# A post-norm decoder layer with a mixture of experts: expert weights split into f16 parts during the attention batches

## What is computed

```python
gate_probs = softmax(x @ gate_w + gate_b)
weights, selected = top_k(gate_probs, 2)
weights = weights / sum(weights)
comb = zeros((n, 8)).at[arange(n)[:, None], selected].set(weights)
h = gelu(einsum('nd,edf->enf', x, w1) + b1[:, None, :])      # w1: 8 x 256 x 1024
expert_out = einsum('enf,efd->end', h, w2) + b2[:, None, :]  # w2: 8 x 1024 x 256
out = einsum('ne,end->nd', comb, expert_out)
```

## Time and profile before

| | before |
|---|---|
| runs, us | 880.97, 886.6, 889.96 (median 886.6) |
| profiled execution, us | 884.88 |
| its span, us | 883.1 |
| mean granted TensorE clock | 0.982 of full speed |
| PE busy | 800.3 us (91%) |
| PEld busy | 608.1 us (69%) |
| DVE busy | 632.6 us (72%) |
| ACT busy | 511.2 us (58%) |
| POOL busy | 260.6 us (30%) |
| chain that ended last | PE 40%, DMA 29%, DVE 10%, SP's queue 7%, ACT 7% |

### The profile page before, as it was taken

One profiled execution on the slowest core, in us unless ns is written; L12 is line 12 of the kernel. 1 busy time (PEld: TensorE's weight loads), 2 busy tenths in 40 slices (PEclk: granted clock), 3 DMA queues, 4 the chain that ended last, 5 costly groups with the idle time before them and its releaser, 6 DMA issues.

```text
span 883.1 us, 30182 instructions
## 1 busy us (share of the span) xinstructions
PE 800.3 (91%) x12379; PEld 608.1 (69%) x12379; DVE 632.6 (72%) x1234; ACT 511.2 (58%) x1084; POOL 260.6 (30%) x334
## 2 busy tenths in 40 slices
PE   5689998999999989999899999999997789999996
PEld 3356766666666666666676666767665569999995
DVE  5866776768777767776777778776864736588887
ACT  2336655666566546655665665656664443687782
POOL 4233223222612251225123421522240103133332
PEclk9999999999999999999999999999999789999999
DMA  7355544554555554554555555545466855766653
GB/s 220 108 149 160 159 137 133 152 164 131 160 148 147 160 149 128 163 152 143 148 151 156 153 158 158 172 136 160 138 190 177 294 195 182 215 202 184 205 155 95
DMA packets 91377, 143.25 MB, mean 162 GB/s; under 512 B 11423, under 2 KB 79583, under 8 KB 87918
## 3 DMA queue, kind: packets, MB, share of 16 engines
q1 hardware_dynamic: 87742, 136.74, 51.8%
q0 software_dynamic: 3504, 4.62, 2.7%
HBM read 101.60 MB, written 39.68 MB: 160 GB/s over the span
## 4 chain that ended last, share of the span: by engine, by line
PE 40%; DMA 29%; DVE 10%; SPq 7%; ACT 7%; issue 5%; DVEq 0%; POOLq 0%; POOL 0%; ACTq 0%
DMA k_dram<-k_two 15%; DMA sums<-y_sb,g_token 9%; PE ps L1613 8%; PE ps L1606 7%; PE ps L1687 5%; SPq L1079 5%; PE ps L1665 4%; DMA k_st<-k_dram 4%; ACT k_two L1368 3%; DVE k_two L507 3%; PE ps L1629 3%; PE ps L1923 3%; DVE negmax L513 2%; PE ps L1944 2%; PE ps L1697 2%
## 5 line engine op out<-in xcount | busy, mean ns | idle before, releaser
L513 DVE TENSOR_REDUCE negmax<-ps 112x1 f32<-112x1500 f32 x121 | 207.3, 1713 | 44.4 <-PE ps L1629 44.1
L1395 ACT ACTIVATE pT<-ps 125x448 f32<-125x448 f32 x384 | 195.8, 546 | 18.6 <-PE ps L1665 14.7
L1230 POOL TENSOR_TENSOR ctx_lo<-ctx_raw,ctx_hi 128x250 f16<-128x250 f32 x188 | 119.3, 666 | 229.7 <-DVE ctx_hi L498 212.8
L1665 PE MATMUL ps<-qbd,k_st 97*128 97x112 f16 x1536 | 129.4, 216 | 20.2 <-ACT qbd L1351 10.8
L1665 PEld LDWEIGHTS ps<-qbd,k_st 97*128 97x128 f16 x1536 | 92.9, 99 | 78.0 <-ACT qbd L1351 27.1
L507 DVE SCALAR_TENSOR_TENSOR k_two<-ps,bk_sb,k_two 128x500 f16<-128x500 f32 x96 | 70.7, 736 | 96.7 <-ACT k_two L1368 96.7
L1368 ACT ACTIVATE k_two<-ps,bk_sb 128x500 f16<-128x500 f32 x96 | 65.1, 678 | 91.6 <-PE ps L1606 68.6
L1351 ACT COPY v_sb<-ps 125x512 f32<-125x512 f32 x96 | 56.3, 587 | 89.5 <-PE ps L1613 89.4
L1687 PE MATMUL ps<-pT,v_sb 125*17 125x56 f32 x6144 | 93.4, 217 | 10.1 <-issue 10.1
L1687 PEld LDWEIGHTS ps<-pT,v_sb 125*17 125x17 f32 x6144 | 81.5, 100 | 29.5 <-issue 19.2
L1629 PE MATMUL ps<-k_st,qbd 96*112 96x500 f16 x363 | 97.4, 375 | 3.7 <-DMA k_st<-k_dram 2.9
(11 more groups left out here) (258 smaller groups left out, 1396.0 us busy)
## 6 DMA issues: line engine op xcount, KB each, us to landing
k_st<-k_dram SPq DMA_DIRECT2D x288, 125.0 KB, 2.6
w_sb<-w SPq DMA_DIRECT2D x25, 1024.0 KB, 5.1
ctx_raw<-ctx_T SPq DMA_DIRECT2D x48, 500.0 KB, 4.5
k_dram<-k_two SPq DMA_DIRECT2D x96, 250.0 KB, 3.6
xs<-zeros SPq DMA_DIRECT2D x28, 260.0 KB, 3.1
w_sb<-w SPq DMA_DIRECT2D x8, 512.0 KB, 4.9
xg<-xs SPq DMA_DIRECT2D x21, 130.0 KB, 4.1
a_x<-x_tok SPq DMA_DIRECT2D x8, 128.0 KB, 2.8
```

The lines of the kernel that those rows point to most:

```text
L513: V.tensor_reduce(negmax[0:QW], ps[0:QW, BANK_S:BANK_S + CHUNKS, 0:MC], AX.XY, ALU.max, negate=True).then_inc(max_done, 1)
L1230: last = nc.gpsimd.tensor_tensor(ctx_lo[:, k, c2, a], ctx_raw[:, k, c2, a], ctx_hi[:, k, c2, a], ALU.subtract)
L1395: nc.scalar.activation(pT[0:MT, (PAIRS * b + p) % 3, TPC * g:TPC * g + TPC], ps[0:MT, BANK_T + n % 2, 0:TPC * QW].rearrange("p (t n) -> p ...
L1665: last = mm(ps[:, BANK_T + n % 2, QW * i:QW * i + QW], k_st[:, j, p, a:a + P], qbd[:, j, p].rearrange("p h s -> p (h s)"), start=True, sto ...
```

## The change: what it does

**Splitting in the batches.** `w1` and `w2` are cut into 32 pieces of 128 x 1024 (`PIECES`). POOL loads a piece (`load_piece`, 512 KB), rounds 32 times its value to f16 (`round_piece`), DVE makes the f16 remainder (`rest_of_piece`), and POOL stores both parts to DRAM (`store_piece`, 512 KB, into `w1_parts` or `w2_parts`). Five pieces go through in each of the first pairs of batches, at slots 2, 4, 8, 10 and 15. There are two buffers for the raw piece, and one, `w_hl`, for its parts: a piece is rounded only when the store of the one before has landed.

**f16 products.** Both layers of every expert tile are sums of three f16 products (high with high, high with low, low with high). The rows are split by DVE into `xgT_hi` and `xgT_lo`, the hidden values by ACT and DVE into `h_hi` and `h_lo`, now for all 21 tiles. `w2_hi_step`, `w2_lo_step` and the f32 second layer are gone. The factor 32 is divided out in the gelu and in the gate.

**Two sums.** Even expert tiles are added to `sums`, odd ones to `sums_odd`; an addition waits for the last one to the same tensor. `sums_odd` is set to zero in the batches, one 128-row tile at a time on SP's queue, loaded at the end into `acc_odd`, and carried into the banks by four more f32 products, two ahead of the last second layer and two behind it.

**Loads.** `w1` has three buffers, and its load waits for the tile three back. In the last batch the loads of `w2` parts are issued between the store of the keys and the wait for it, not behind the loads of the keys. The order of the first five expert tiles on PE and DVE is written anew.

```diff
@@ POOL @@
+            def round_piece(n):
+
+                if n < len(PIECES):
+                    pool.wait_ge(raw_in[n % 2], 16 * (n // 2 + 1))
+                    if n > 0:
+                        pool.wait_ge(w_parts_out, 16 * n)
+                    nc.gpsimd.tensor_scalar(w_hl[:, 0], w_raw[:, n % 2], W_UP, None, ALU.mult).then_inc(w_hi_made, 1)
+
+            def store_piece(n):
+
+                if n < len(PIECES):
+                    of, e, i = PIECES[n]
+                    pool.wait_ge(w_lo_made, n + 1)
+                    nc.gpsimd.dma_start((w1_parts if of == 1 else w2_parts)[e, i],
+                                        w_hl[:].rearrange("p i n -> p (i n)")).then_inc(w_parts_out, 16)
+                if n + 2 < len(PIECES):
+                    load_piece(n + 2)
...
             def add(g):
                 pool.wait_ge(row_read, g + 1)
                 pool.wait_ge(y_ready, g + 1)
-                if g > 0:
-                    pool.wait_ge(added, 16 * g)
+                if g > 1:
+                    pool.wait_ge(added[g % 2], 16 * (g // 2))
...
@@ DVE @@
+            def rest_of_piece(n):
+
+                if n < len(PIECES):
+                    dve.wait_ge(w_hi_made, n + 1)
+                    V.scalar_tensor_tensor(w_hl[:, 1], w_raw[:, n % 2], W_UP, w_hl[:, 0], ALU.mult, ALU.subtract).then_inc(w_lo_made, 1)
...
-                V.tensor_copy(xgT[:, g % 2], ps[:, XG_BANK, 0:D].rearrange("p (c n) -> p c n", c=CH)).then_inc(xgT_done, 1)
+                src = ps[:, XG_BANK, 0:D].rearrange("p (c n) -> p c n", c=CH)
+                V.tensor_copy(xgT_hi[:, g % 2], src).then_inc(xgT_done, 1)
+                dve.wait_ge(xgT_done, 2 * g + 1)
+                V.tensor_tensor(xgT_lo[:, g % 2], src, xgT_hi[:, g % 2], ALU.subtract).then_inc(xgT_done, 1)
...
@@ SP @@
-            def keys(b, par, u):
+            def keys(b, par, u, between=()):
...
                 sp.dma_start(k_dram[i], k_two[:, i]).then_inc(k_out[g], 16)
+                for dst, src in between:
+                    sp.dma_start(dst, src).then_inc(w2_in, 16)
                 sp.wait_ge(k_out[g], 16 * (CHUNKS * b + c + 1))
...
-                if g >= 2:
-                    sp.wait_ge(m1_done, 2 * g - 2)
+                if g >= 3:
+                    sp.wait_ge(m1_done, 2 * g - 4)
...
@@ PE @@
                 for q in range(4):
                     f = 4 * i + q
-                    for c in range(CH):
-                        last = mm(ps[:, H_BANK + 2 * par + i, P * q:P * q + P],
-                                  w1_sb[:, par, c, P * f:P * f + P], xgT[:, par, c],
-                                  start=(c == 0), stop=(c == CH - 1))
+                    for n, (x, w) in enumerate(SPLIT):
+                        for c in range(CH):
+                            last = mm(ps[:, H_BANK + 2 * par + i, P * q:P * q + P],
+                                      w1_place(g)[:, c, F * w + P * f:F * w + P * f + P], (xgT_hi, xgT_lo)[x][:, par, c],
+                                      start=(n == 0 and c == 0), stop=(n == 2 and c == CH - 1))
...
+                pe.wait_ge(h_lo_done, g + 1)
                 for f in range(FT):
...
+                    for n, (x, w) in enumerate(SPLIT):
+                        a = F * w + D * (f % 4)
+                        last = mm(ps[:, Y_BANKS[par], 0:D], (h_hi, h_lo)[x][:, par, f],
+                                  w2_sb[:, bass.ds(e, 1), f // 4, a:a + D].rearrange("p a n -> p (a n)"),
+                                  start=(f == 0 and n == 0), stop=(f == FT - 1 and n == 2))
...
+            for q in (2, 3):
+                carried_odd(q)
+            m2(GT - 1)
```

More of the change, by code:

```diff
@@ L360, in decoder_layer @@
         row_made = sem("row_made")
-        w2_hi_done = sem("w2_hi_done")
-        w2_lo_done = sem("w2_lo_done")
+        raw_in = [sem(f"raw_in{k}") for k in range(2)]
+        w_hi_made = sem("w_hi_made")
+        w_lo_made = sem("w_lo_made")
+        w_parts_out = sem("w_parts_out")
+        odd_in = sem("odd_in")
         h_hi_done = sem("h_hi_done")
@@ L376, in decoder_layer @@
         b2_in = sem("b2_in")
-        added = sem("added")
+        added = [sem(f"added{k}") for k in range(2)]
         gate_step = sem("gate_step")
@@ L417, in decoder_layer, with w1_place @@
         C_FREE = (9 - UNITS, 0, 4)
+        PIECE_AT = {2: 0, 4: 1, 8: 2, 10: 3, 15: 4}
         W2_AHEAD = (1, 2, 1, 1, 2, 1)
+        PIECES = [(2, e, i) for e in range(E // 2) for i in range(2)] + [(1, e, i) for e in range(E) for i in range(CH)] \
+            + [(2, e, i) for e in range(E // 2, E) for i in range(2)]
+        def w1_place(g):
+            return w1_third if g % 3 == 2 else w1_sb[:, g % 3]
         def home(k, t):
@@ L825, in batch @@
                     at_slot = PAIRS * j + slot
+                    piece = PIECE_AT.get(at_slot, len(PIECES)) + 5 * t if t_next is not None else len(PIECES)
                     ak = A_AT_DVE.get(at_slot, -1)
@@ L849, in batch @@
                         b_tail(bt, t_before)
+                    if at_slot == 4:
+                        rest_of_piece(piece)
                     if units_on:
@@ L1137, in _ @@
             two_batches(TILES - 2, last=True)
+            ahead = [(e, i) for e in range(E // 2) for i in range(2)]
+            sp.wait_ge(a_qlo_done, 2 * TILES)
+            sp.wait_ge(a_x1_kept, TILES)
+            sp.wait_ge(w_parts_out, 16 * E)
+            for u, pieces in zip(KEY_UNITS, W2_AHEAD):
+                keys(B - 1, 1, u, [(w2_sb[:, e, i], w2_parts[e, i]) for e, i in ahead[:pieces]])
+                ahead = ahead[pieces:]
+            sp.wait_ge(unit_done, UNITS * B)
+            sp.wait_ge(ctx_lo_done, CHUNKS * B)
+            sp.wait_ge(w_parts_out, 16 * len(PIECES))
+            for e in range(E // 2, E):
+                sp.dma_start(w2_sb[:, e], w2_parts[e].rearrange("i p n -> p i n")).then_inc(w2_in, 16)
             sp.dma_start(xs_tiles[E * REGION:].rearrange("g p n -> p g n"),
@@ L1140, in _ @@
             sp.dma_start(sums_tiles[TILES], zeros[:, 0:D]).then_inc(sums_set, 16)
-            half = FT // 2
-            ahead = [(e, f) for e in range(E // 2) for f in (0, half)]
-            sp.wait_ge(a_qlo_done, 2 * TILES)
-            sp.wait_ge(a_x1_kept, TILES)
-            for u, pieces in zip(KEY_UNITS, W2_AHEAD):
-                keys(B - 1, 1, u)
-                for e, f in ahead[:pieces]:
-                    sp.dma_start(w2_sb[:, e, f:f + half], w2[e, :, f:f + half]).then_inc(w2_ahead, 16)
-                ahead = ahead[pieces:]
-            sp.wait_ge(unit_done, UNITS * B)
-            sp.wait_ge(ctx_lo_done, CHUNKS * B)
-            for e in range(E // 2, E):
-                sp.dma_start(w2_sb[:, e], w2[e]).then_inc(w2_in, 16)
+            for t in (TILES - 1, TILES):
+                sp.dma_start(odd_tiles[t], zeros[:, 0:D]).then_inc(sums_set, 16)
             keep_x2(TILES - 2, TILES - 1)
@@ L1178, in _ @@
             sp.dma_start(b2_all[:], b2.unsqueeze(0).to_broadcast([P, E, D])).then_inc(b2_in, 16)
-            for g in range(2, EARLY):
+            sp.wait_ge(st_done, CHUNKS * PAIRS * B)
+            load_w1(2)
+            load_xg(2)
+            for g in range(3, EARLY):
                 load_xg(g)
@@ L1317, in add @@
                 pool.wait_ge(y_ready, g + 1)
[L1318 to L1319 removed]
+                if g > 1:
+                    pool.wait_ge(added[g % 2], 16 * (g // 2))
                 nc.gpsimd.indirect_dma_start(
[L1321 to L1322 removed]
+                    out=sums_odd if g % 2 else sums, out_offset=bass.IndirectOffsetOnAxis(ap=g_token[:, g % 4:g % 4 + 1], axis=0),
+                    in_=y_sb[:, g % 2], in_offset=None, compute_op=ALU.add).then_inc(added[g % 2], 16)
             iteration(0, None)
@@ L2015, in spread @@
                         last.then_inc(hot_done, 1)
+            carried_odd(0)
+            carried_odd(1)
             carried(0)
```

205 lines of the change are left out of this document (103 added, 102 removed).

## The result

The changed kernel takes 951.3 us (median of 4 runs, 943.7 to 954.8) against 883.8 us (4 runs, 878.2 to 890.0) for the kernel before on the same chip: ratio 1.075, 95% interval 1.069 to 1.080. Forecast were 876 us, with 862 to 893 as range and 0.15 for slower. It is slower by 67 us. No rival named a time near it; only the open end of rival C, "896 and up" with a chance of 0.07, contains it. Medians and ranges, here and in the table of the experiments, are over all runs of a kernel, and the ratios with their intervals compare only its fast runs with fast ones, because some runs of one and the same kernel are 1.5% and more above its fastest.

The account below looks back on a forecast made before the run. PE bounds the expert tiles, level with the additions to `sums` in late ones; the keys' trip to DRAM and back leads the batches' chain. 884.9 - 12.1 - 2.5 - 2 + 8 = 876.3, so 876 us, range 862 to 893.

Parts of the forecast that it names:

- rival C: Batches give the gain back through key stores meeting pieces and late POOL: 884 to 895 us, chance 0.18; slower part 0.07.
- DMA: In the batches, ten pieces per pair rarely meet the six or so chain stores: 0.7 us per pair lost, 0 to 2.9.
- Slot 4: In the batches, POOL's rounding of 1.4 us makes DVE's remainder end slightly late: 0.3 us per pair lost, 0 to 1.3.
- Holds between DVE and POOL: In the batches, roundings on POOL and work on DVE hold each other up: 0.2 us per pair lost.
- Sum of the batches: Splitting pieces costs 1.2 us per pair over 6.4 pairs: 8 us lost, bounds 0 and 32.
- First layer: In expert tiles, 48 f16 products at 57 ns take 2.74 us instead of 3.57: 0.83 us gained per tile.
- Rival D: The expert tiles' first layer gets slower, 84 ns per product against a break-even of 74: 903 us, chance 0.08.
- Second layer: In expert tiles, 24 f16 products take 2.63 us: 0.21 us gained per late tile, 0.83 per early tile.
- Late tiles: Sixteen late expert tiles at 5.59 us each, less costs at the end: 12.1 us gained, bounds 7 and 16.
- the odd sums: At the end, PE waits 2 us for the new acc_odd before the last second layer.
- Early tiles: First five expert tiles: 8.3 us taken from PE, less five waits of about 1.2 us: 2.5 us gained, 0 to 8.3.
- Last batch: Loads of w2 stand behind the keys' store, not ahead of the next one: 2 us gained, 0 to 4.

Follow-up runs that it names:

- dma_only: The changed kernel with all loads and stores of pieces, but rounding and remainder left out after the first piece: 948.0 us, 1.068 of before.
- no_pieces: The changed kernel with all but the first piece's loads, rounding, remainder and stores left out; experts load that one piece: 868.9 us, 0.977 of before.
- free_none: no_pieces with the keys' loads reading a fixed unit and not waiting for the keys' store, every byte kept: 841.7 us, 0.956 of before.
- compute_only: no_pieces with rounding and remainder of all pieces kept, but later piece transfers cut to one row: 897.8 us, 1.014 of before.
- compute_dve: compute_only with the rounding moved from POOL to DVE: 872.9 us, 0.988 of before.
- before_order: The kernel before, with only the last batch's w2 loads moved between the keys' store and the keys' loads: 874.9 us, 0.993 of before.
- free_dma: dma_only with the keys' loads reading a fixed unit and not waiting for the keys' store, every byte kept: 875.4 us, 0.992 of before.

## Why the prediction was wrong, step by step

- **DMA, "0.7 us per pair, from 0 to 2.9": the step that failed.** dma_only shows 10.5 us per pair over no_pieces (94.9 against 84.4). The step asked how often a piece meets one of "the six or so stores on the chain". But all twelve trips of a pair stand one behind the other in SP's queue, and together with what they wait for they fill the pair (in free_none the pair gets shorter when the trips do, and SP's slack of 48.7 us took up nothing of the longer stores). So every store is as good as on the chain; each landed 0.8 us later, not one in four by half of 2.9. Nor does the 0.7 follow from these terms: one in four of six stores, by half of 2.9 us, is 2.2 us per pair, and one in four of ten pieces is 3.6. With 2.2 the forecast would have been some 886 us. The prediction had both figures in its rows: 2.19 and 5.04 us for a store. It treated a long serial trip as a few meetings. It also had no price for the clock, which fell behind such a wait, and none for the pauses of PE. Of the 81 us of the transfers, 33 stay when the trip is taken out.
- **Slot 4, "with 1.4 us it ends at 415.4", 0.3 us per pair.** The rounding takes 2.77 us, beyond even the upper bound of 2.3. compute_only shows 3.3 us per pair (87.6 against 84.4), compute_dve 1.2. The slope between rows of two-input operations on few columns did not give one-input cost on 1024. Holds between DVE and POOL (0.2 forecast) are in this 3.3: in the trace of the changed kernel the 14 casts of the context that take 0.86 us and more all stand beside an instruction of POOL, and the other 34 take 0.67 us. They are not all the rounding's: the cast of 3.57 us stood beside `a_kbd`, which is in the kernel before too, and free_none, without roundings behind the first, has one of 3.31.
- **Sum of the batches, 8 us (0 to 32).** 12.5 us in each of six pairs, and 79.7 us at the last maximum; over 120 to 640 us the granted clock fell from 1.00 to 0.96. Rival C named both mechanisms (stores meet pieces; POOL late in slot 4), but priced them at 3 us per pair, or 4.4 and up, and gave them 0.25 together.
- **First layer, 57 ns a product: right.** 2.68 us per tile. Rival D falls: in a stream of 24 with a weight load each a product takes 56 ns (1.34 us / 24), under its break-even of 74.
- **Second layer, 2.63 us: right** (2.62).
- **Late tiles, 12.1 us gained.** Tiles 5.53 us apart (5.59 forecast). From the first late tile to the end, the change gained 121.4 - 113.0 = 8.4 us, but 121.4 - 108.2 = 13.2 in no_pieces (from 755.6 to 863.8 us); with 1.1 us in the early tiles that is 14.3, where 12.1 + 2.5 = 14.6 were forecast. The experts' loads of no_pieces read one piece over and over; what that is worth was not measured. The rest of the difference is at the end: the odd sums were forecast to cost PE 2 us of wait, and did cost 2.74 us, or 1.55 in no_pieces. Behind the longer wait the granted clock is 0.58 for 3.3 us, and four products take 3.28 us where the next four take 1.88 in the same view; behind the shorter one it stays at 1.00, and they take 1.98:

```profile
926.21 3.28 PE L2016 MATMUL ps<-acc_odd,id 128*128 128x512 f32 x4 [2.74 <-DMA acc_odd<-sums_odd]
```

```profile
844.21 1.98 PE L2019 MATMUL ps<-acc_odd,id 128*128 128x512 f32 x4 [1.55 <-DMA acc_odd<-sums_odd]
```

- **Early tiles, 2.5 us gained: near by its number, half by its mechanism.** 40.1 - 38.3 = 1.8 us, and 1.1 in no_pieces; PE waits 1.0 to 1.5 us five times. The step put all five down to the split of the hidden values ahead of the second layer. Only the first and the last are that (1.20 and 1.31 us, ended by DVE's `h_lo`). The three between stand ahead of the first layer (1.02, 1.53 and 1.49 us), where PE cannot start before DVE has made both parts of the rows, the "one small subtraction" that the prediction had put at nothing; that the sum came near is partly luck. In the one of 1.53 us (PE, then DVE) the low part is there at 818.23 us, and PE starts at 818.34:

```profile
818.34 0.38 PE L1985 MATMUL ps<-xgT_hi,w_sb 128*128 128x128 f16 x4 [1.53 <-issue]
817.81 0.42 DVE L949 TENSOR_TENSOR xgT_lo<-ps,xgT_hi 128x256 f16<-128x256 f32 x1
```

- **Last batch, 2 us gained (0 to 4).** The order alone is worth 6.3 us in before_order. It was under-sized. In the changed kernel, too, the last 16 intervals are 2.6 us shorter than before (80.7 against 83.3) and the way from the last maximum to the first expert matmul 3.3 us (37.1 against 40.4): 5.9 us together. In no_pieces that last way is 34.0 us; where the further 3.1 us come from was not looked into.

What stays open: why PE pauses more with the pieces, which by the two traces can be 16.4 of the 33 us of free_dma over free_none. The rest can lie in longer context loads (4.9 against 4.0 us in the median), in the keys' loads (4.6 against 3.0 us) and in the clock (0.99 against 1.00 over 120 to 640 us); no run tells them apart.

## What to carry to other kernels

Before traffic is added "in idle bandwidth", ask how many dependent round trips stand one behind another in a queue, and whether they fill the period. Here they did, and the added bytes were paid in latency: with the transfers alone a store of keys landed 0.8 us later (3.09 to 3.89 us) and a pair grew by 10.5 us, though the DMA share was 0.53 without them. Multiply the delay of one trip by all trips, not by those that the chain happened to name. And first shorten the trip: here giving a buffer back at its store instead of at its loads, with the order of one batch, gained 2.8% where the change lost 7.5%.
